# First tiles of K: one tile's statistics early, tile 0 split from TensorE's bank, tokens normalized in place, and another closing of the block

## The chip, the cores and the metric

The kernel runs on one core of one Trainium2 chip. The metric is the device time of one execution in microseconds, lower is better. All numbers below are of the kernel before the change.

## The reference

One transformer layer on 2048 tokens of width 512: a linear attention with 32 heads of 64, then a mixture of 8 experts of which each token takes two. The change touches the first part, the normalization of the tokens and the projection and accumulation of K.

```python
def attn(x, Wq, Wk, Wv, Wo, bo):              # x: [2048, 512], already normalized
    q = relu(x @ Wq); k = relu(x @ Wk); v = x @ Wv      # [2048, 32 * 64]
    kv = einsum('bhsd,bhse->bhde', k, v)                # sum over the tokens
    qkv = einsum('bhsd,bhde->bhse', q, kv)
    normalizer = clip(einsum('bhsd,bhd->bhs', q, k.sum(axis=tokens)), 1e-06, None)
    return (qkv / normalizer) @ Wo + bo

x = x + attn(layernorm(x), ...)               # layernorm: (x - mean) / sqrt(var + 1e-5)
x = x + moe(layernorm(x), ...)                # gates: softmax of the top 2 of 8 scores
# moe: h = silu(x @ w1[e].T + b1[e]); y = h @ w2[e].T + b2[e]; out = sum of gate * y
```

## The kernel before, in words

The tokens lie in 16 tiles of 128 tokens by 512. Everything is float32, and TensorE takes each product as three matmuls of rounded halves: each operand is split into a rounded part (`_hi`, made by ScalarE) and the difference to it (`_lo`, made by VectorE), and `three` (lines 1633 to 1636) issues hi x hi, hi x lo and lo x hi.

Instead of V and K'V the kernel accumulates A = xn' K over the tokens, and multiplies by Wv later. K has 2048 columns, taken in four chunks of 512. For each tile in a chunk, `project_k` (line 1652) gives 12 matmuls into a bank of pK, ScalarE and VectorE make k_hi and k_lo of it, and `accumulate_at` (line 1663) adds 12 matmuls to the four banks of pA. The first chunk also makes the operands: per tile VectorE takes statistics (`stats`: BATCH_NORM_STATS2 and BATCH_NORM_AGGREGATE), ScalarE the root (`sqrt_var`), VectorE refines its reciprocal in four small steps (`newton_rstd`) and normalizes (`normalize`, line 1206). TensorE transposes the tile into the bank pT (`transpose_xn`, line 1644), ScalarE copies it to xnT (`put_xnT`) and rounds the copy (`split_xnT`), VectorE subtracts. ScalarE and VectorE also split the untransposed tile (`split_xn`) and blocks of Wk (`split_wk`).

The order on every engine is written out by hand, with semaphores between the engines. For the first chunk `chunk0_pair` (line 1688) gives TensorE's order: project tile n + 1, transpose tile n + 2, accumulate tile n. Pairs 1 to 6 are a loop on TensorE (line 1703), pairs 0 and 7 stand apart. VectorE's order at the start is in lines 1256 to 1269, ScalarE's in lines 864 to 883. `keep_clock` issues transposes whose result nobody reads.

The normalized tile goes to xn_new (two buffers), and GpSimd copies it back over the tile in xn (`keep_xn`, line 587), which xn_kept tells. ScalarE's `split_xn` waits for that copy; VectorE waits for the copy and the transposes of the tile two before, ahead of writing the buffer again (line 1213).

SyncE's queue loads tile 0 of the tokens (semaphore s_first), four blocks of Wk, then tiles 1 to 3 (all on s_x[0], line 418), three small tensors of biases (s_b), and the other twelve tiles.

At the other end the experts' results are added to the output by GpSimd's DMAs (`add_out`, line 711, 39 of them, the last from y_last); SyncE waits for the last two of each parity (lines 563 and 564). The block (`nc.Block()`, line 396) closes with a drain on each engine and a barrier of all five.

## Time and profile before

| | us |
|---|---|
| median of 3 runs | 1025.12 (1024.0 to 1026.88) |
| profiled execution, its own time | 1023.68 |
| its span, first to last instruction | 1021.7 |
| TensorE busy | 998.7 |
| VectorE, ScalarE, GpSimd busy | 689.6, 515.1, 267.5 |
| granted TensorE clock, mean | 0.996 |

Busy time of TensorE counts overlapping matmuls once; a matmul of 512 columns is shown as 0.39 long, and one starts 0.23 after the other. A name such as pA<-k_hi,xn_hi is output<-inputs. In brackets stands how long the engine was idle ahead of the row and what ended it. PEq, POOLq and SPq are the sequencers of TensorE, GpSimd and SyncE; drains, semaphore instructions and branches are theirs and count as no busy time.

### The profile page before, as it was taken

What the parts mean: (1) busy time and instruction counts of PE and PEld (TensorE: products, weight loads), DVE (VectorE), ACT (ScalarE), POOL (GpSimd) and SP (SyncE); (2) the same over time, 40 slices, a digit from 0 to 9 for tenths busy, and PEclk for the clock granted to TensorE, in tenths of its full rate; (3) what the DMA queues carried; (4) which work ended last, traced back from release to release, by engine and by line L of the source; (5) the groups of instructions that cost most, each with busy time, mean ns of one, the idle gap of its engine ahead of it and who ended that gap; (6) DMA issues with size and microseconds to landing.
All of it is one profiled execution on the core that took longest, in us unless ns stands there. A gap on an engine that the chain in (4) does not pass through costs nothing.

```text
span 1021.7 us, 17596 instructions
## 1 busy us (share of the span) xinstructions
PE 998.7 (98%) x5029; PEld 841.5 (82%) x5030; DVE 689.6 (68%) x1555; ACT 515.1 (50%) x1325; POOL 267.5 (26%) x432
## 2 busy tenths in 40 slices
PE   8999999999999999999999999999999989999995
PEld 7777888888888888888788888888888879989984
DVE  6888665565566667667877887788877754444442
ACT  4445444444444447755555555555555953333331
POOL 2000000000000002223323333333224645555553
PEclk9999999999999999999999999999999999999998
DMA  7012500100000011343111111111136725565642
GB/s 259 1 41 82 206 21 21 41 21 21 21 21 22 21 63 63 103 172 114 49 45 52 41 41 41 41 41 43 39 100 183 207 64 100 106 104 100 113 90 33
DMA packets 46858, 75.31 MB, mean 74 GB/s; under 512 B 6089, under 2 KB 18554, under 8 KB 46690
## 3 DMA queue, kind: packets, MB, share of 16 engines
q1 hardware_dynamic: 37010, 56.04, 17.7%
q0 software_dynamic: 9808, 18.79, 10.0%
q8 instruction: 18, 0.29, 0.1%
q14 instruction: 22, 0.18, 0.1%
HBM read 53.14 MB, written 23.50 MB: 75 GB/s over the span
## 4 chain that ended last, share of the span: by engine, by line
PE 90%; DVE 5%; ACT 2%; issue 1%; DMA 1%; SPq 0%; POOLq 0%; ACTq 0%; DVEq 0%
PE pK L1634 15%; PE pK L1636 15%; PE pK L1635 15%; PE pA L1634 6%; PE pA L1635 6%; PE pA L1636 6%; PE pX L1634 6%; PE pX L1636 5%; PE pX L1635 5%; PE pA L1769 3%; PE pT L1979 2%; PE pT L1715 2%; PE pA L1903 1%; PE pX L1997 1%; PE pK L1903 1%
## 5 line engine op out<-in xcount | busy, mean ns | idle before, releaser
L983 ACT ACTIVATE qs<-q,nrec 128x64 f32<-128x64 f32 x512 | 129.6, 335 | 89.0 <-DVE nrec L1359 89.0
L1634 PE MATMUL pA<-k_hi,xn_hi 128*128 128x512 f32 x256 | 101.2, 395 | 1.2 <-DVE xn_lo L1217 0.7
L1634 PE MATMUL pK<-wk_hi,xnT_hi 128*128 128x512 f32 (+1 forms) x256 | 100.0, 391 | 0.7 <-DVE xnT_lo L1217 0.7
L1634 PE MATMUL pK<-wq_hi,xnT_hi 128*128 128x512 f32 x256 | 100.4, 392 | 0.0
L1636 PE MATMUL pK<-wq_hi,xnT_lo 128*128 128x512 f32 x256 | 99.9, 390 | 0.0
L1635 PE MATMUL pA<-k_lo,xn_hi 128*128 128x512 f32 x256 | 99.8, 390 | 0.0
L1635 PE MATMUL pK<-wk_lo,xnT_hi 128*128 128x512 f32 (+1 forms) x256 | 99.7, 390 | 0.0
L1636 PE MATMUL pA<-k_hi,xn_lo 128*128 128x512 f32 x256 | 99.7, 389 | 0.0
L1636 PE MATMUL pK<-wk_hi,xnT_lo 128*128 128x512 f32 (+1 forms) x256 | 99.6, 389 | 0.0
L1635 PE MATMUL pK<-wq_lo,xnT_hi 128*128 128x512 f32 x256 | 99.6, 389 | 0.0
L1634 PE MATMUL pX<-m_hi,qsT_hi 128*128 128x512 f32 x240 | 99.0, 413 | 0.0
L1636 PE MATMUL pX<-m_hi,qsT_lo 128*128 128x512 f32 x240 | 94.2, 392 | 0.0
L1635 PE MATMUL pX<-m_lo,qsT_hi 128*128 128x512 f32 x240 | 93.7, 390 | 0.0
L1352 DVE TENSOR_TENSOR qs<-q,ksum 128x512 f32<-128x512 f32 x64 | 51.8, 810 | 55.1 <-ACT q L977 55.1
L603 POOL TENSOR_TENSOR wv_lo<-wv_in,wv_hi 128x512 fp32r<-128x512 f32 x4 | 5.2, 1293 | 313.6 <-ACT wo_hi L904 313.6
L727 POOL DMA_INDIRECT out<-y,slot_token x38 | 65.8, 1732 | 69.4 <-DVE y L1600 44.1
L1237 DVE SCALAR_TENSOR_TENSOR k_lo<-pK,k_hi 128x512 fp32r<-128x512 f32 x64 | 44.1, 689 | 56.4 <-ACT k_hi L853 56.4
L847 ACT CAST xn_hi<-xn 128x512 fp32r<-128x512 f32 x64 | 39.6, 619 | 67.5 <-PE pA L1636 67.4
L977 ACT ACTIVATE q<-pK 128x512 f32<-128x512 f32 x64 | 38.2, 597 | 67.8 <-PE pK L1636 67.7
L853 ACT ACTIVATE k_hi<-pK 128x512 fp32r<-128x512 f32 x64 | 38.0, 594 | 66.5 <-PE pK L1636 66.5
L1158 ACT ACTIVATE hT<-pX,b1T 128x128 f32<-128x128 f32 (+1 forms) x117 | 34.1, 363 | 72.0 <-PE pX L1997 72.0
L1217 DVE TENSOR_TENSOR xn_lo<-xn,xn_hi 128x512 fp32r<-128x512 f32 x64 | 45.6, 712 | 27.4 <-ACT xn_hi L847 27.4
(283 smaller groups left out, 2464.7 us busy)
## 6 DMA issues: line engine op xcount, KB each, us to landing
w_in<-in_ffn_w SPq DMA_DIRECT2D x22, 256.0 KB, 3.6
w_in<-in_ffn_w SPq DMA_DIRECT2D x8, 704.0 KB, 7.4
xn<-in_attn_hidden_states SPq DMA_DIRECT2D x16, 256.0 KB, 5.9
wv_in<-in_attn_Wv SPq DMA_DIRECT2D x16, 256.0 KB, 2.7
wo_in<-in_attn_Wo SPq DMA_DIRECT2D x16, 256.0 KB, 2.9
wk_in<-in_attn_Wq SPq DMA_DIRECT2D x4, 1024.0 KB, 5.7
xnT_dram<-xnT SPq DMA_DIRECT2D x4, 1024.0 KB, 11.5
x_in<-in_attn_hidden_states SPq DMA_DIRECT2D x16, 256.0 KB, 2.6
```

The costliest lines, as they stand in the source:

```text
L727: pool.indirect_dma_start(out, bass.IndirectOffsetOnAxis(slot_token[:, i:i + 1].bitcast(U32), 0), rows, None, bounds_check=T - 1, oob_is_e ...
L847: nc.scalar.copy(xn_hi[:, b * D:(b + 1) * D], xn[:, ds(t * D, D)]).then_inc(xn_hi_ready, 1)
L853: nc.scalar.activation(k_hi[:, b * CW:(b + 1) * CW], pK[:, b * 512:(b + 1) * 512], ACT.Relu).then_inc(k_hi_ready, 1)
L977: nc.scalar.activation(q[:, b * CW:(b + 1) * CW], pK[:, b * 512:(b + 1) * 512], ACT.Relu).then_inc(q_ready, 1)
L983: i = nc.scalar.activation(qs[:, s], q[:, s], ACT.Copy, scale=nrec[:, b * HC + h:b * HC + h + 1])
L1158: last = nc.scalar.activation(hT[0:w, b * P:(b + 1) * P], pX[0:w, b * P:(b + 1) * P], ACT.Silu, bias=b1T[0:w, ds(b * E + e, 1)])
L1217: return nc.vector.tensor_tensor(dst, src, f(hi), ALU.subtract)
L1237: nc.vector.scalar_tensor_tensor(out=k_lo[:, s], in0=pK[:, b * 512:(b + 1) * 512], scalar=0.0, in1=f(k_hi[:, s]), op0=ALU.max, op1=ALU.sub ...
L1352: nc.vector.tensor_tensor(qs[:, b * CW:(b + 1) * CW], q[:, b * CW:(b + 1) * CW], ksum[:, c * CW:(c + 1) * CW], ALU.mult).then_inc(qk_ready, 1)
L1634: nc.tensor.matmul(dst, lhs[0], rhs[0], start=start, stop=False)
L1635: nc.tensor.matmul(dst, lhs[0], rhs[1], start=False, stop=False)
L1636: return nc.tensor.matmul(dst, lhs[1], rhs[0], start=False, stop=stop)
```

## The change

1. Tile 1 gets a semaphore of its own (s_second), and s_x[0] counts tiles 2 and 3 alone. VectorE takes tile 1's statistics between the third and the fourth block of Wk, and normalizes it behind the fourth. Tile 2's statistics and its normalization are parted in the same way, around tile 1's xnT_lo.
2. Tile 0: ScalarE rounds xnT_hi from the bank pT, VectorE takes the difference from the bank, and ScalarE's copy to xnT comes after both.
3. All tiles are normalized in place in xn. xn_new, GpSimd's copy and the semaphore xn_kept are gone; TensorE transposes from xn, and ScalarE waits for xn_ready.
4. TensorE transposes the biases ahead of tile 1 instead of behind it, and its loop over pairs 1 to 6 becomes straight code.
5. The block is made with `no_gpsimd_drain=True`. GpSimd waits for the last adds itself and issues `dma_reset()`. In the built program that is a drain marked as a reset, which names the semaphores 96 to 255; the other engines' drains now stand ahead of the barrier's own instructions, and GpSimd has none but the reset.

```diff
-    xn_new = sb("xn_new", 2 * D, 168 * KB)
...
+        s_second = sem("s_second")
...
-        xn_kept = sem("xn_kept")
...
-        block = ctx.enter_context(nc.Block())
+        block = ctx.enter_context(nc.Block(no_gpsimd_drain=True))
...
-                    sp.dma_start(xn[:, t * D:(t + 1) * D], x[t * P:(t + 1) * P, :]).then_inc(s_x[g] if t else s_first, 16)
+                    sp.dma_start(xn[:, t * D:(t + 1) * D], x[t * P:(t + 1) * P, :]).then_inc(s_x[g] if t > 1 else (s_first, s_second)[t], 16)
...
-            def keep_xn(t, b):
-                pool.wait_ge(xn_ready, t + 1)
-                pool.tensor_copy(xn[:, ds(t * D, D)], xn_new[:, b * D:(b + 1) * D]).then_inc(xn_kept, 1)
...
-            keep_xn(0, 0)
-            keep_xn(1, 1)
-            keep_xn(2, 0)
-            keep_xn(3, 1)
-            with pool.Fori(2, NT // 2) as p:
-                for b in range(2):
-                    keep_xn(2 * p + b, b)
...
+            pool.wait_ge(s_add[0], 16 * (NS // 2 + 1))
+            pool.wait_ge(s_add[1], 16 * (NS // 2))
+            pool.dma_reset()
...
             split_wk(0, 1)
+            act.wait_ge(xnT_put, 1)
+            nc.scalar.copy(xnT_hi[:, 0:D], pT[:, :]).then_inc(xnT_hi_ready, 1)
+            split_wk(0, 2)
+            act.wait_ge(xnT_lo_ready, 1)
             put_xnT(0)
-            split_xnT(0, 0, 0)
-            split_wk(0, 2)
             split_wk(0, 3)
             sqrt_var(1)
-            act.wait_ge(xn_kept, 1)
+            act.wait_ge(xn_ready, 1)
...
-                    act.wait_ge(xn_kept, n + 1)
+                    act.wait_ge(xn_ready, n + 1)
...
             def layernorm1(t, b):
                 stats(xn[:, ds(t * D, D)], t)
+                normalize1(t)
+
+            def normalize1(t):
                 newton_rstd(t)
-                if not (isinstance(t, int) and t < 2):
-                    dve.wait_ge(xnT_put, t - 1)
-                    dve.wait_ge(xn_kept, t - 1)
-                normalize(xn_new[:, b * D:(b + 1) * D], xn[:, ds(t * D, D)]).then_inc(xn_ready, 1)
+                normalize(xn[:, ds(t * D, D)], xn[:, ds(t * D, D)]).then_inc(xn_ready, 1)
...
-            split_xnT(0, 0, 0)
+            dve.wait_ge(xnT_hi_ready, 1)
+            lo(xnT_lo[:, 0:D], pT[:, :], xnT_hi[:, 0:D]).then_inc(xnT_lo_ready, 1)
             split_wk(0, 2)
+            dve.wait_ge(s_second, 16)
+            stats(xn[:, D:2 * D], 1)
             split_wk(0, 3)
-            dve.wait_ge(s_x[0], 48)
-            layernorm1(1, 1)
+            normalize1(1)
             split_xn(0, 0, 0)
             split_k(0, 0)
-            layernorm1(2, 0)
+            dve.wait_ge(s_x[0], 32)
+            stats(xn[:, 2 * D:3 * D], 2)
             split_xnT(1, 1, 1)
+            normalize1(2)
             add_k(0, 0, 0)
...
-                    last = nc.tensor.transpose(pT[:, i * P:(i + 1) * P], xn_new[:, b * D + i * P:b * D + (i + 1) * P], ident[:, :])
+                    last = nc.tensor.transpose(pT[:, i * P:(i + 1) * P], xn[:, t * D + i * P:t * D + (i + 1) * P], ident[:, :])
...
-            transpose_xn(1, 1)
             pe.wait_ge(s_b, 48)
...
+            transpose_xn(1, 1)
...
-            with pe.Fori(1, 7) as p:
+            for p in range(1, 8):
                 chunk0_pair(p)
-            chunk0_pair(7)
```

ScalarE at the start of the program, before; rs is the scratch of the root, wk_in a raw block of Wk:

```order
L834 COPY xnT<-pT 128x512 [waits xnT_put]
L842 CAST xnT_hi<-xnT 128x512 [waits xnT_ready]
L826 CAST wk_hi<-wk_in 128x512 [waits s_wk02]
L826 CAST wk_hi<-wk_in 128x512 [waits s_wk03]
L830 ACTIVATE rs<-mv,eps 128x1 [waits var_ready]
L847 CAST xn_hi<-xn 128x512 [waits xn_kept]
```

ScalarE at the same place in the changed program:

```order
L860 CAST xnT_hi<-pT 128x512 [waits xnT_put]
L817 CAST wk_hi<-wk_in 128x512 [waits s_wk02]
L825 COPY xnT<-pT 128x512 [waits xnT_put,xnT_lo_ready]
L817 CAST wk_hi<-wk_in 128x512 [waits s_wk03]
L821 ACTIVATE rs<-mv,eps 128x1 [waits var_ready]
L838 CAST xn_hi<-xn 128x512 [waits xn_ready]
```

The rounding of tile 0 stands first and reads pT; the copy to xnT has moved behind the third block of Wk and waits for VectorE's difference.

VectorE from its first difference of tile 0 to the k_lo of tile 0, before; the BN rows are statistics, the rows on rs refine the reciprocal:

```order
L1217 TENSOR_TENSOR xnT_lo<-xnT,xnT_hi 128x512 [waits xnT_hi_ready]
L1217 TENSOR_TENSOR wk_lo<-wk_in,wk_hi 128x512 [waits wk_hi_ready] x2
L1200 BN_STATS st_117<-xn 128x6 [waits s_x0]
L1203 BN_AGGR mv<-st_117 128x2 [waits bn_stats_done]
L1190 RECIPROCAL rs<-rs 128x1 [waits sqrt_ready]
L1192 TENSOR_SCALAR rs<-mv,rs 128x1 [waits rstd_step]
L1194 TENSOR_SCALAR rs<-rs 128x1 [waits rstd_step]
L1196 TENSOR_SCALAR rs<-rs 128x1 [waits rstd_step]
L1206 TENSOR_SCALAR xn_new<-xn,mv,rs 128x512 [waits rstd_step]
L1217 TENSOR_TENSOR xn_lo<-xn,xn_hi 128x512 [waits xn_hi_ready]
L1237 SCALAR_TENSOR_TENSOR k_lo<-pK,k_hi 128x512 [waits k_hi_ready]
```

VectorE at the same place in the changed program:

```order
L1210 TENSOR_TENSOR xnT_lo<-pT,xnT_hi 128x512 [waits xnT_hi_ready]
L1210 TENSOR_TENSOR wk_lo<-wk_in,wk_hi 128x512 [waits wk_hi_ready]
L1193 BN_STATS st_116<-xn 128x6 [waits s_second]
L1196 BN_AGGR mv<-st_116 128x2 [waits bn_stats_done]
L1210 TENSOR_TENSOR wk_lo<-wk_in,wk_hi 128x512 [waits wk_hi_ready]
L1183 RECIPROCAL rs<-rs 128x1 [waits sqrt_ready]
L1185 TENSOR_SCALAR rs<-mv,rs 128x1 [waits rstd_step]
L1187 TENSOR_SCALAR rs<-rs 128x1 [waits rstd_step]
L1189 TENSOR_SCALAR rs<-rs 128x1 [waits rstd_step]
L1199 TENSOR_SCALAR xn<-xn,mv,rs 128x512 [waits rstd_step]
L1210 TENSOR_TENSOR xn_lo<-xn,xn_hi 128x512 [waits xn_hi_ready]
L1230 SCALAR_TENSOR_TENSOR k_lo<-pK,k_hi 128x512 [waits k_hi_ready]
```

Tile 1's statistics have moved ahead of the fourth block of Wk and wait for s_second; the four rows on rs and the normalization stay behind it, and the normalization writes xn itself.

TensorE between the projection and the first accumulation of tile 0, before:

```order
L1635 MATMUL pK<-wk_lo,xnT_hi 128x512
L1636 MATMUL pK<-wk_hi,xnT_lo 128x512
L1649 MATMUL pT<-ident,xn_new 128x128 [waits xnT_ready,xn_ready]
L1649 MATMUL pT<-ident,xn_new 128x128 x3
L1682 MATMUL pX<-ident,gw_in 128x8 [waits s_b]
L1682 MATMUL pX<-ident,gw_in 128x8 x3
L1685 MATMUL pX<-ident,b_in 128x8 x2
L1685 MATMUL pX<-ident,b_in 96x8
L1686 MATMUL pX<-ident,b_in 128x32
L1634 MATMUL pA<-k_hi,xn_hi 128x512 [waits k_lo_ready,xn_lo_ready]
```

TensorE at the same place in the changed program:

```order
L1632 MATMUL pK<-wk_lo,xnT_hi 128x512
L1633 MATMUL pK<-wk_hi,xnT_lo 128x512
L1678 MATMUL pX<-ident,gw_in 128x8 [waits s_b]
L1678 MATMUL pX<-ident,gw_in 128x8 x3
L1681 MATMUL pX<-ident,b_in 128x8 x2
L1681 MATMUL pX<-ident,b_in 96x8
L1682 MATMUL pX<-ident,b_in 128x32
L1646 MATMUL pT<-ident,xn 128x128 [waits xnT_ready,xn_ready]
L1646 MATMUL pT<-ident,xn 128x128 x3
L1631 MATMUL pA<-k_hi,xn_hi 128x512 [waits k_lo_ready,xn_lo_ready]
```

The transposes of the biases (gw_in, b_in) come first, and tile 1's, which wait for VectorE, directly ahead of the accumulation.

## Rows read from the trace of the kernel before

**Rows 1.** The page: span, and busy time of each engine over it.

```profile
span 1021.7 us, 17596 instructions
PE 998.7 (98%) x5029; PEld 841.5 (82%) x5030; DVE 689.6 (68%) x1555; ACT 515.1 (50%) x1325; POOL 267.5 (26%) x432
```

**Rows 2.** Instructions of the block's end, line 227: engine, operation, duration ns, start us.

```profile
L227 POOLq DRAIN  x1: 9617/9617/9617, 1011.8 to 1011.8; - x1
L227 SPq COMPARE_BRANCH  x1: 38/38/38, 1014.7 to 1014.7; - x1
L227 POOLq EVENT_SEMAPHORE  x2: 17/17/17, 1021.5 to 1021.6; - x2
```

**Rows 3.** SyncE's own waits from 1000 us on: total us, times, longest.

```profile
SPq L227 <- PEq L227: 6.7, 1, 6.7
```

**Rows 4.** Instructions of the program's start, line 2053, on GpSimd's queue.

```profile
L2053 POOLq INC_SWDGE_SEM  x1: 31/31/31, 0.2 to 0.2; - x1
L2053 POOLq DRAIN  x1: 174/174/174, 0.4 to 0.4; - x1
```

**Rows 5.** Section 6 of the page: GpSimd's DMA issues by tile, with counts.

```profile
xg<-xn_dram,slot_token POOLq DMA_INDIRECT x39, 4.2
out<-y,slot_token POOLq DMA_INDIRECT x38, 4.9
meta_dram<-vals,slot_i POOLq DMA_INDIRECT x32, 2.6
```

**Rows 6.** Timeline of the first tiles: start us, us, engine, line, operation, count, idle before.

```profile
7.15 0.59 ACT L834 COPY xnT<-pT 128x512 f32<-128x512 f32 x1 [0.28 <-PE pT L1649]
7.77 0.62 ACT L842 CAST xnT_hi<-xnT 128x512 fp32r<-128x512 f32 x1
8.42 0.69 DVE L1217 TENSOR_TENSOR xnT_lo<-xnT,xnT_hi 128x512 fp32r<-128x512 f32 x1 [0.45 <-ACT xnT_hi L842]
9.17 0.50 PE L1634 MATMUL pK<-wk_hi,xnT_hi 128*128 128x512 f32 x1 [0.74 <-DVE xnT_lo L1217]
10.70 0.69 DVE L1200 BATCH_NORM_STATS2 st<-xn 128x6 f32<-128x512 f32 x1 [0.38 <-DMA xn<-in_attn_hidden_states]
12.42 0.59 ACT L853 ACTIVATE k_hi<-pK 128x512 fp32r<-128x512 f32 x1
12.99 0.55 DVE L1206 TENSOR_SCALAR xn_new<-xn,mv,rs 128x512 f32<-128x512 f32 x1
13.59 0.66 PE L1649 MATMUL pT<-ident,xn_new 128*128 128x128 f32 x4 [1.41 <-DVE xn_new L1206]
14.05 0.68 DVE L1237 SCALAR_TENSOR_TENSOR k_lo<-pK,k_hi 128x512 fp32r<-128x512 f32 x1
14.88 0.47 PE L1634 MATMUL pA<-k_hi,xn_hi 128*128 128x512 f32 x1
```

**Rows 7.** Busy time in one stretch: length, PE, PEld, DVE, ACT, POOL, clock, DMA share, GB/s.

```profile
9.00:10.00 1.00, 0.83 (x4) 0.70 (x5) 1.00 (x3) 0.43 (x1) 0.00 (x0) 1.00 1.07 377
```

**Rows 8.** Timeline of TensorE in the first chunk of K, transposes and accumulations.

```profile
24.44 0.50 PE L1634 MATMUL pA<-k_hi,xn_hi 128*128 128x512 f32 x1
36.09 0.60 PE L1649 MATMUL pT<-ident,xn_new 128*128 128x128 f32 x4
36.83 0.50 PE L1634 MATMUL pA<-k_hi,xn_hi 128*128 128x512 f32 x1
42.45 0.60 PE L1649 MATMUL pT<-ident,xn_new 128*128 128x128 f32 x4
42.89 0.50 PE L1634 MATMUL pA<-k_hi,xn_hi 128*128 128x512 f32 x1
98.77 0.50 PE L1634 MATMUL pA<-k_hi,xn_hi 128*128 128x512 f32 x1
```

**Rows 9.** Timeline around one copy by GpSimd, VectorE's difference beside it.

```profile
29.30 0.62 POOL L589 COPY xn<-xn_new 128x512 f32 x1 [5.46 <-DVE xn_new L1206]
29.64 0.81 DVE L1217 TENSOR_TENSOR xn_lo<-xn,xn_hi 128x512 fp32r<-128x512 f32 x1
```

## The prediction

> **What bounds the kernel now.** I read the page first: the span is 1021.7 us and TensorE is busy for 998.7 of it [rows 1]. So nothing that another engine does in the middle can be worth much, and what TensorE does not fill has to be found at the two ends and in waits. The instructions of the block's last line come next, since the span does not end with the last computation: GpSimd's queue holds a DRAIN of 9617 ns from 1011.8, and the barrier that closes the program follows it at 1021.5 [rows 2]. SyncE has seen all adds to the output land by 1014.7, when it branches to the end [rows 2]; it then waits 6.7 us for the barrier [rows 3]. That view names TensorE as the releaser; what came last is the drain. The third view is the timeline of the first tiles, where the reader is to see ScalarE copy the transposed tile twice, one after the other, before TensorE starts on K at 9.17, and VectorE start tile 1's statistics only at 10.70, when three tiles are in, with the first accumulation at 14.88 behind them [rows 6]. The fourth is TensorE in the first chunk of K: transposes at 36.09 and 42.45, accumulations at 36.83 and 42.89 [rows 8]. The first of those two starts 0.74 after its transposes, the second 0.44: every other step waits for VectorE.
>
> My sum is made against the profiled execution's own time, 1023.68 us (its span and 1.98 around it). The median of the three runs shown is 1025.12, 1.44 above it; I take the sum off both alike.
>
> **Tile 0 split from TensorE's bank.** Before, the transposed tile is copied to SBUF in 0.59, the copy rounded in 0.62, and VectorE's difference starts at 8.42, 0.69 long [rows 6]. Now ScalarE rounds straight from the bank and VectorE subtracts from the bank. I give both the durations of the nearest rows (0.59 for a read of that bank by ScalarE, 0.68 for VectorE's reading of a bank in the k_lo row). TensorE starts about 0.64 earlier, at 8.53. The copy to SBUF is still made, but behind the difference, and nobody waits for it before tile 1's transposes. By itself this is worth nothing: the accumulation waits for tile 1's statistics too, as they stand ahead of xn_lo and k_lo on VectorE.
>
> **Tile 1's statistics early.** They wait for one tile, not three. Three were in at 10.70 less a few hundredths [rows 6]; the queue moves 377 GB/s then [rows 7], 0.70 us for a tile of 262,144 bytes, so tile 1 should be in two tiles earlier, near 9.28. From statistics to normalization VectorE needs 12.99 - 10.70 = 2.29 [rows 6]; the fourth block of Wk is now subtracted in between, in about 0.6, most of it while ScalarE takes the root, which I count as 0.2. Normalization starts at 9.28 + 2.29 + 0.2 = 11.77, 1.22 before 12.99. xn_lo, k_lo and the accumulation follow as before, if k_hi is there: it came 12.42 - 9.17 = 3.25 behind TensorE's start [rows 6], so now at 11.8 to 11.9 and 0.59 long, ahead of k_lo at 12.83. TensorE has the bias transposes and tile 1's (0.66 us [rows 6]) done by then. First accumulation: 14.88 - 1.22 = 13.66. Behind it VectorE takes tile 2's statistics, tile 1's xnT_lo, then normalizes tile 2; its end near 16.5 meets TensorE, free 2.85 after 13.66. So the 1.2 us stays. Bounds: nothing, if tile 1 lands with tile 3; 1.5 us, if it is in by 9.0. I take 1.2. POOL's copy of tile 0, for which ScalarE's xn_hi waited, is gone as well, but was done long before.
>
> **Normalized in place.** Fifteen more steps lose GpSimd's copy. Its row matters because it overlaps VectorE's xn_lo: the copy runs from 29.30 to 29.92, and the difference from 29.64 takes 0.81 against 0.69 for one that no copy meets [rows 9, 6]. [...] That difference ends a chain: from transposes at 36.09 to the accumulation after next at 42.89 are 6.80, and from 36.83 to the next transposes at 42.45 are 5.62 [rows 8]; 6.80 + 5.62 = 12.42 is the period of a pair, and (98.77 - 24.44) / 6 = 12.39 the measured one [rows 8]. With 0.13 less in the chain a pair takes 12.27. TensorE's own work, 2 x (5.62 + 0.44) = 12.12, stays below that. Six pairs give 6 x 0.13 = 0.8 us. Bounds: 0, if the normalization in place pays it back; 1.6 (6 x 0.27), if the chain falls under TensorE's own work. The waits that VectorE drops before normalizing had been met earlier.
>
> **TensorE's loop unrolled.** Steps 1 to 7 of the pair loop become straight code. Accumulations keep their distance over the loop's edges (the measured pair is the chain's), so the branch costs nothing that shows: 0. SyncE's queue keeps its order and its issues.
>
> **Closed without a drain.** The plain drain goes. In its place GpSimd waits for the adds (in at 1014.7) and then does a reset, of a form that the trace does not have. Of the 9.6 us, 1011.8 to 1014.7 are cover for the transfer and stay; 6.7 are not [rows 2, 3]. A drain with no DMA behind it took 0.17 at the start [rows 4]; the one at the end follows 109 and two more DMAs [rows 5], so its 6.7 us may be some 60 ns for each. The reset costs between 0.17 and 6.7. I take 1.0, near the lower row, because what it could wait for has landed. Saved: 5.7 us.
>
> **Sum.** 1.2 + 0.8 + 5.7 = 7.7. Profiled execution: 1023.68 - 7.7 = 1016.0, span 1014.0. Median of runs: 1025.12 - 7.7 = 1017.4.
>
> **Rivals.** (1) The reset costs what the drain cost, or the clearing of the queue's records moves behind the span into the 1.98 us around it. For it: the 60 ns per DMA may be bookkeeping that any ending must do. Against it: the reset is issued when nothing is outstanding. Saved 1.2 + 0.8 = 2.0, time 1023.1: no change. [...]
> (2) Slower: the reset does the drain's walk and clears semaphores one by one besides. With 6.7 for the walk and 31 ns for each of the 160 semaphores that the built reset names, the length of the one instruction on semaphores of that queue [rows 4], it takes 11.7, 5.0 over the drain; less 2.0 from the front that is 1028.1. It turns slower once the reset exceeds 6.7 + 2.0 = 8.7. Against it: it would have to cost more than what it replaces.
> (3) The front doesn't move, because tile 1 lands late or TensorE, with VectorE's new order, waits for the fourth block of Wk (due there at 10.9, ready near 10.9): saved 0.8 + 5.7 = 6.5, time 1018.6. The range of the forecast covers it.
>
> **Chances.** A measurement of this kernel can tell about 0.3%, 3.1 us, from no change. My forecast, with (3) inside it: 0.80, from 1015.5 (reset 0.17, front 1.5, chunk 1.5, a microsecond of scatter) to 1021.5 (reset 3, front 0.5). Rival (1): 0.16. Rival (2): 0.04. Faster by over 0.3%: 0.80; within: 0.16; slower: 0.04. The range from 1015.0 to 1022.5 leaves out a good part of (1), all of (2) and the edges of the first.
>
> **What would show it.** On GpSimd's queue one DRAIN that starts after the last landing, about 2.9 us after where the old one started, and lasts 1.0; the span ends 0.3 behind it. First projection matmul near 8.5, first accumulation near 13.7, statistics of tile 1 near 9.3. xn_lo at 0.69 throughout, no copy on GpSimd, the pair at 12.27 and the last transposed step's accumulation near 96.8. A reset over 4 us, or a time around the span far above 1.98, would make the forecast wrong; so would new idle time of TensorE in the unrolled steps.

## The result, and the profile after

The changed kernel takes 1015.14 us (median of 4 runs, 1014.65 to 1015.29) against 1026.0 us for the kernel before beside it (4 runs, 1024.0 to 1027.16). The ratio is 0.990, 95% interval 0.9886 to 0.9914. The profiled execution took 1015.22 us, 8.46 less than that of before, with 1.72 us around its span. I had forecast 1016.0 for it and 1017.4 for the median, with a range from 1015.0 to 1022.5: the measured median lies only 0.14 above the range's lower end.

The page of the changed kernel, to be read against [rows 1]: the span is 8.2 us shorter, and TensorE is busy for the same time.

```profile
span 1013.5 us, 17496 instructions
...
PE 998.8 (99%) x5029; PEld 841.7 (83%) x5030; DVE 686.7 (68%) x1555; ACT 515.4 (51%) x1325; POOL 256.4 (25%) x416
```

The end comes first, since the largest term was there. These are instructions by source line (engine queue, operation, count, duration in ns, start in us). The reset on line 806 answers to the DRAIN of [rows 2]:

```profile
L806 POOLq DRAIN  x1: 293/293/293, 1013.0 to 1013.0; - x1
...
L226 POOLq EVENT_SEMAPHORE  x2: 17/17/17, 1013.3 to 1013.4; - x2
...
L226 SPq COMPARE_BRANCH  x1: 43/43/43, 1013.0 to 1013.0; - x1
```

VectorE's last work, first in the kernel before and then in the changed one:

```profile
1010.51 0.75 DVE L1628 TENSOR_SCALAR y_last<-pA,slot_gate 128x512 f32<-128x512 f32 x1 [1.74 <-PE pA L1636]
```

```profile
1008.72 0.75 DVE L1625 TENSOR_SCALAR y_last<-pA,slot_gate 128x512 f32<-128x512 f32 x1 [1.74 <-PE pA L1633]
```

It starts 1.79 us earlier, so 1.8 us of the 8.2 come from the front and the middle. The remaining 6.4 come from the end: the reset starts when the last add is in, lasts 0.29 us, and the barrier follows at 1013.3, where the old drain held it until 1021.5.

The timeline of the first tiles, against [rows 6]:

```profile
9.06 0.50 PE L1631 MATMUL pK<-wk_hi,xnT_hi 128*128 128x512 f32 x1
...
9.53 0.69 DVE L1193 BATCH_NORM_STATS2 st<-xn 128x6 f32<-128x512 f32 x1
...
11.93 0.55 DVE L1199 TENSOR_SCALAR xn<-xn,mv,rs 128x512 f32<-128x512 f32 x1
...
12.99 0.68 DVE L1230 SCALAR_TENSOR_TENSOR k_lo<-pK,k_hi 128x512 fp32r<-128x512 f32 x1
...
13.82 0.47 PE L1631 MATMUL pA<-k_hi,xn_hi 128*128 128x512 f32 x1 [0.52 <-DVE k_lo L1230]
```

TensorE starts on K at 9.06 (9.17 before), tile 1's statistics at 9.53 (10.70), its normalization at 11.93 (12.99), and the first accumulation at 13.82 (14.88), 1.06 earlier. This is one pair of executions. The five profiled executions with this front (the changed kernel, e2, e3, e9, e10) have the first accumulation at 13.10 to 14.21, the five with the old front (before, e1, e4, e5, e8) at 14.88 to 15.64.

TensorE's accumulations in the first chunk, against [rows 8], and VectorE once beside them:

```profile
23.50 0.50 PE L1631 MATMUL pA<-k_hi,xn_hi 128*128 128x512 f32 x1
...
32.90 0.18 DVE L1196 BATCH_NORM_AGGREGATE mv<-st 128x2 f32<-128x6 f32 x1 [0.54 <-DVE st L1193]
...
36.19 0.50 PE L1631 MATMUL pA<-k_hi,xn_hi 128*128 128x512 f32 x1 [0.54 <-DVE xn_lo L1210]
...
42.12 0.48 PE L1631 MATMUL pA<-k_hi,xn_hi 128*128 128x512 f32 x1
...
97.51 0.50 PE L1631 MATMUL pA<-k_hi,xn_hi 128*128 128x512 f32 x1
```

From 42.12 to 97.51 the pairs take 12.25 to 12.28 us, as forecast. The first full pair, 23.50 to 36.19, takes 12.69: TensorE waits 0.54 for xn_lo, because VectorE stood still for 0.54 before it aggregated its statistics at 32.90, with no releaser but its own last instruction. At the end of the chunk the changed kernel is 98.77 - 97.51 = 1.26 ahead, and it stays 1.25 to 1.27 ahead until 717 us.

The rest of the 1.8 appears where the expert stage begins. This row of before and the one of the changed kernel are the same transposes of w_in; "issue" means that TensorE waited for nothing that the profile shows:

```profile
817.48 0.63 PE L1903 MATMUL pK<-ident,w_in 128*128 128x128 f32 x4 [1.23 <-issue]
```

```profile
815.66 0.63 PE L1899 MATMUL pK<-ident,w_in 128*128 128x128 f32 x4 [0.29 <-issue]
```

TensorE's unexplained wait shrinks from 1.23 to 0.29. At VectorE's last work the changed kernel is 1.79 ahead, 0.53 more than in the stages before this one.

### The profile page after: what moved, and what is told of

It reads as the page before. It is cut to its first block, busy times and chain, and to the rows that moved or that the text cites. A ratio compares the mean times of both kernels' runs of the same rounds, so it can differ in the third digit from the quotient of the medians.

```text
span 1013.5 us, 17496 instructions
## 1 busy us (share of the span) xinstructions
PE 998.8 (99%) x5029; PEld 841.7 (83%) x5030; DVE 686.7 (68%) x1555; ACT 515.4 (51%) x1325; POOL 256.4 (25%) x416
## 3 DMA queue, kind: packets, MB, share of 16 engines
HBM read 53.14 MB, written 23.50 MB: 76 GB/s over the span
## 4 chain that ended last, share of the span: by engine, by line
PE 91%; DVE 5%; ACT 2%; issue 1%; DMA 0%; POOL 0%; ACTq 0%; DVEq 0%; POOLq 0%
PE pK L1631 15%; PE pK L1633 15%; PE pK L1632 15%; PE pA L1631 6%; PE pA L1632 6%; PE pA L1633 6%; PE pX L1631 6%; PE pX L1633 5%; PE pX L1632 5%; PE pA L1765 3%; PE pT L1975 2%; PE pT L1711 2%; PE pA L1899 1%; PE pX L1993 1%; PE pK L1899 1%
## 6 DMA issues: line engine op xcount, KB each, us to landing
wk_in<-in_attn_Wq SPq DMA_DIRECT2D x4, 1024.0 KB, 5.8
xnT_dram<-xnT SPq DMA_DIRECT2D x4, 1024.0 KB, 11.7
```

## The experiments

Time is the median over the runs; the interval is that of the ratio to the kernel before, run on the same chip alongside. The kernel before itself came to 1025.13 (23 runs, 1023.28 to 1028.51) beside e1 to e4, 1024.64 (23 runs, 1023.13 to 1026.88) beside e5 to e8, and 1024.77 (9 runs) beside e9 to e12. The letters A to I name the theories in the expectation that stands ahead of each result.

```
                                     time us   range               runs  ratio interval
e1  before, only the end changed     1018.14   1016.70 to 1019.65   6    0.9910 to 0.9946
e2  changed, plain drain back        1020.82   1020.31 to 1022.27   6    0.9936 to 0.9970
e3  changed, waits and plain drain   1022.55   1021.87 to 1024.44  12    0.9965 to 0.9988
e4  before, only in place            1023.80   1022.11 to 1024.98  12    0.9973 to 0.9996
e5  before, only the loop unrolled   1024.48   1022.44 to 1025.33  12    0.9983 to 1.0004
e6  changed, statistics 1 late       1017.39   1015.84 to 1018.47   6    0.9915 to 0.9940
e7  changed, tile 0 through SBUF     1014.78   1014.71 to 1015.04   4    0.9888 to 0.9917
e8  before, TensorE kept busy        1024.74   1022.92 to 1025.03  11    0.9990 to 1.0007
e9  changed, drains in the loop      1020.85                        1    (profiled run)
e10 changed, no reset                1014.40   1013.98 to 1014.93   5    0.9884 to 0.9915
e11 e6, TensorE kept busy            1015.83   1015.24 to 1016.38   5    0.9897 to 0.9928
e12 e7, no reset, tile 1 first       1014.78   1014.40 to 1015.73   5    0.9889 to 0.9921
```

### The end: e1, e2, e3, e9, e10

**e1, the kernel before with only its end changed.**

```diff
-        block = ctx.enter_context(nc.Block())
+        block = ctx.enter_context(nc.Block(no_gpsimd_drain=True))
...
                 add_out(i)
+            pool.wait_ge(s_add[0], 16 * (NS // 2 + 1))
+            pool.wait_ge(s_add[1], 16 * (NS // 2))
+            pool.dma_reset()
```

> The kernel before with only its end changed: GpSimd waits for the adds, resets its DMA state, and the block closes without the plain drain. Theory A (the three parts add up, the end is worth what the two traces differ by there): SyncE's branch to the barrier is followed by 0.3 to 0.5 us instead of 6.7, so the span falls by 6.4, from 1021.7 to about 1015.3, and the time of an execution like the profiled one from 1023.7 to 1017.3. The first 1008 us are as before. Rival B (the scatter of the kernel before, 1024.0 to 1027.2, sits in its drain, whose length varies): the median falls by more than 6.4, from 1026.0 to about 1017.3, and the runs lie within 0.7 us. Rival C (the scatter sits elsewhere): the median falls by 6.4, to 1019.6, and the runs stay 3 us apart.

Measured: span 1015.0 in the profiled execution, against 1015.3 expected, and 7.0 off the median. The rows by source line:

```profile
L818 POOLq DRAIN  x1: 303/303/303, 1014.5 to 1014.5; - x1
...
L227 POOLq EVENT_SEMAPHORE  x2: 17/17/17, 1014.8 to 1014.9; - x2
...
L227 SPq COMPARE_BRANCH  x1: 43/43/43, 1014.5 to 1014.5; - x1
```

The reset takes 0.30 here too, and the end alone is worth 6.4 to 7.0. But the runs stay 3 us apart, so B falls: most of the scatter of the kernel before is not in its drain. With it comes a clue, TensorE's mean granted clock of each run:

```
e1 runs, us (clock): 1016.70 (1.0)   1016.73 (1.0)   1017.89 (0.998)
                     1018.39 (0.997) 1018.53 (0.997) 1019.65 (0.995)
```

**e2, the changed kernel with the plain drain back** (the reverse edit).

> The changed kernel with only its end undone: plain drain, no waits for the adds, no reset. Theory A: the drain on GpSimd's queue starts near 1010 and lasts 9.6 us again, the span is 1013.5 + 6.4 = 1019.9, the time 1021.6, 2.1 below the profiled execution of before and 4 below its median if the drain varies from run to run as before does (then up to 1025). Rival D (the early part of the change also shortens the drain, because GpSimd has 16 copies fewer behind it): drain under 8 us, time below 1020.5.

Measured: 1020.82, 5.7 above the changed kernel; the profiled execution is the longest of the six (1022.27, 7.05 above the one of the changed kernel). The drain and what follows the branch are as before (D falls):

```profile
L226 POOLq DRAIN  x1: 9722/9722/9722, 1010.6 to 1010.6; - x1
L226 SPq COMPARE_BRANCH  x1: 38/38/38, 1013.6 to 1013.6; - x1
```

**e3, the two waits kept, but a plain drain behind them.**

```diff
             pool.wait_ge(s_add[1], 16 * (NS // 2))
-            pool.dma_reset()
```

(and `nc.Block()` as before.)

> The changed kernel with its two waits for the adds kept, and a plain drain where the reset was. The drain now starts when all has landed, at 1013.0. Theory E (a plain drain does a fixed piece of work for the DMAs of the program, about 60 ns for each, whenever it is issued): 9.6 us long, span 1023, time 1024.5 to 1025. Theory F (that work went on beside the landing only in part: the 6.7 us begin when the last transfer lands): 6.7 us long, span 1020.1, time 1021.8, as without the waits. Rival G (what made the drain long was that it was issued with a transfer in flight; the waits cure it, not the reset): 0.3 us long, span 1013.5, time 1015.2 as the changed kernel.

Measured: 1022.55, 7.4 above the changed kernel.

```profile
L226 POOLq COMPARE_BRANCH  x1: 41/41/41, 1012.7 to 1012.7; - x1
...
L226 POOLq DRAIN  x1: 7835/7835/7835, 1012.9 to 1012.9; - x1
```

Everything has landed at 1012.7, and the plain drain still takes 7.8. So G falls: it is the kind of closing, not the waiting, that is cheap. The number lies between E and F: of the drain's own work of 7.8 us about 1.1 ran beside the transfer in the kernel before, where 6.7 stayed uncovered [rows 2, 3]. The twelve runs of e3 spread over 2.6 us at mean clocks of 0.995 and 0.996, where those of the changed kernel spread over 0.6. So some scatter comes back with the plain drain as well; which part of the program it sits in, no profile here shows.

**e9, plain drains in the routing loop as well.**

```diff
                     put_slots(2 * h + (b - 2), b)
+                    pool.drain()
```

(the end as in e2.)

> The changed kernel with the plain drain at the end again and no waits or reset, and twelve plain drains more on GpSimd, one behind the two DMAs of each step of the routing loop, where GpSimd then idles for 7 us. The last drain comes behind 111 DMAs in all and 83 since the drain before it. Theory A (about 60 ns for each DMA issued since the last drain): the drains in the loop last for their two DMAs' landing and little more, all alike, 2 to 2.5 us, and the last one's uncovered part falls from 6.7 to 83 x 0.06 = 5.0. Theory B (60 ns for each DMA ever issued): the drains in the loop grow by 0.12 us from one to the next, 1.4 us over the twelve, and the last is as long as before, 9.6. Theory C (a fixed price for any plain drain that has had a software DMA before it, whatever their number): each lasts 8 to 10 us, the loop's idle time does not hide them, and the time goes up by 10 us or more.

Measured, the twelve drains of line 688 (shortest, median, longest) and the end:

```profile
L688 POOLq DRAIN  x12: 3399/3939/8017, 517.3 to 779.6; - x12
...
L226 POOLq DRAIN  x1: 8454/8454/8454, 1010.4 to 1010.4; - x1
L226 SPq COMPARE_BRANCH  x1: 38/38/38, 1013.4 to 1013.4; - x1
```

The drains in the loop have two DMAs each to wait for. In order they take 3.9, 3.6, 3.6, 4.0, 3.4, 3.8, 3.6, 4.3, 4.3, 4.6, 5.0 and 8.0 us, so C, a fixed price of 8 to 10, falls. The last drain is uncovered from 1013.4 to 1018.9, 5.5 us, against 6.7 without the drains before it: by that B falls, and A (5.0) comes near. The last drain is shorter when earlier ones stand in the loop. But the drains in the loop are longer than I expected and not all alike: from the first to the eleventh they grow by 1.2 us, as much as B gives, and 5.5 is more than a strict proportion gives. It is a single run. That the drain's work is proportional to the DMAs since the last one is not shown, and why the twelfth is longest stays open.

**e10, no reset either.**

```diff
             pool.wait_ge(s_add[1], 16 * (NS // 2))
-            pool.dma_reset()
```

> The changed kernel without the reset: GpSimd waits for the adds and joins the barrier, with neither drain nor reset. Theory A: the reset's 0.29 us was all that stood between the last landing and the barrier, so the time falls by 0.2 to 0.3, to 1014.9. Rival B: SyncE's own way to the barrier (branch at 1013.0, its event at 1013.2) sets the end as much, and it falls by less than 0.15. Rival C: what the reset cleared is then cleared behind the span: the span falls by 0.3 and the time around it, 1.7 us, grows.

```profile
L226 POOLq EVENT_SEMAPHORE  x2: 17/17/17, 1012.8 to 1012.9; - x2
...
L226 SPq COMPARE_BRANCH  x1: 43/43/43, 1012.5 to 1012.5; - x1
```

From the branch to the span's end it is 0.5 us with and without the reset (1013.0 to 1013.5, 1012.5 to 1013.0). B holds: SyncE's own way to the barrier hides most of the 0.29. The time around the span is 1.73, as with the reset (1.72), so C falls. The median is 0.74 below the changed kernel's, which was not run beside it; but in the profiled execution the branch itself comes 0.5 earlier: that difference does not lie at the end. The ratio to before, 0.9884 to 0.9915, is that of the changed kernel.

### The first tiles and the scatter: e6, e7, e8, e11, e12

**e6, tile 1's statistics late again.**

```diff
+            split_wk(0, 3)
             dve.wait_ge(s_second, 16)
+            dve.wait_ge(s_x[0], 32)
             stats(xn[:, D:2 * D], 1)
-            split_wk(0, 3)
             normalize1(1)
```

> The changed kernel with only tile 1's statistics put back behind the fourth block of Wk and behind the landing of all of the first four tiles. Theory A (my term for the early statistics): normalization of tile 1 near 13.0, first accumulation near 14.9, 1.1 later than in the changed kernel, time of a good execution 1016.2. Theory C (the kernels with the old first tiles lie up to 4 us apart in their runs and show a lower mean clock in the slower ones, because TensorE idles for 1.4 us before tile 1's transposes and sometimes loses its clock there): the scatter comes back, 1016.2 to 1019, mean clock 0.995 to 0.999, median near 1017.5. Rival D (the scatter belongs to tile 0's way through SBUF, TensorE's idle 0.74 before the first projection): no scatter here, runs within 0.7 us.

Measured: first accumulation at 15.09, 1.27 later than in the changed kernel, and the scatter is back; even the fastest run is 0.7 above the changed kernel's median. TensorE's rows with idle time, and its windows (length, busy, clock, DMA share, GB/s):

```profile
13.80 0.66 PE L1647 MATMUL pT<-ident,xn 128*128 128x128 f32 x4 [1.48 <-DVE xn L1199]
15.09 0.47 PE L1632 MATMUL pA<-k_hi,xn_hi 128*128 128x512 f32 x1 [0.64 <-DVE k_lo L1230]
...
15.00:16.00 1.00, 0.91 (x4) 0.91 1.05 385
16.00:17.00 1.00, 1.00 (x4) 0.50 1.06 389
17.00:18.00 1.00, 1.00 (x3) 0.50 1.09 375
18.00:20.00 2.00, 2.00 (x10) 0.69 1.06 370
```

This profile shows what those of before and of the changed kernel don't: TensorE is at 0.50 of full speed for 0.2 + 2.0 + 1.2 = 3.4 us from 15.8 on, after 1.48 us and 0.64 us of idling; from 20 on it is at 1.00 again. From 15.87 to 18.86 a matmul of 512 columns starts 0.42 to 0.43 us after the one before it; in e11, at 1.00, 0.22 to 0.24. I estimate the work lost at half of the 3.4, 1.7 us. In the profiles of before and e1, the clock is 1.00 in the same windows after idle stretches of 1.41 and 1.04. The kernel with only the loop unrolled (e5) shows it too, after 2.00 us:

```profile
14.35 0.66 PE L1649 MATMUL pT<-ident,xn_new 128*128 128x128 f32 x4 [2.00 <-DVE xn_new L1206]
...
16.00:17.00 1.00, 1.00 (x5) 0.80 1.07 391
17.00:18.00 1.00, 1.00 (x4) 0.50 1.08 360
18.00:20.00 2.00, 2.00 (x6) 0.50 1.06 375
```

**e11, e6 with that idle stretch filled** by ten transposes of the identity that nobody waits for.

```diff
+            keep_clock(10)
             transpose_xn(1, 1)
```

> The kernel of the late statistics (tile 1's statistics behind the fourth block and the four tiles), with ten more transposes of the identity for TensorE, 1.25 us, in the idle stretch before tile 1's transposes. Theory C (in the executions at 1016.6 to 1018.5 TensorE ran at half clock for about 3 us after that idle stretch): with the stretch filled the clock stays and the slow executions go: median 1015.9 instead of 1017.4, runs from 1015.6 to 1016.5, first accumulation still near 15.0. Rival D (the clock falls for another reason, or the idle 0.64 before the first accumulation is enough): median 1017 or more, with the half clock at 16 to 20 us still there.

```profile
13.79 0.66 PE L1647 MATMUL pT<-ident,xn 128*128 128x128 f32 x4 [0.45 <-DVE xn L1199]
...
16.00:17.00 1.00, 1.00 (x6) 1.00 1.06 387
17.00:18.00 1.00, 1.00 (x6) 1.00 1.09 365
18.00:20.00 2.00, 2.00 (x12) 1.00 1.06 373
```

The first accumulation is at 15.08, as in e6, but the clock stays up and the median falls by 1.56 to 1015.83. The two were measured on different chips, with five and six runs, and their ratio intervals touch (0.9897 to 0.9928 and 0.9915 to 0.9940). What supports C beside the medians is the mean clock: 0.999 to 1.0 in all five runs of e11, 0.997 to 0.999 in the six of e6. So for this kernel C is well supported: with the statistics late, most of what makes executions longer than 1016.4 is the half clock after the idle stretch. All runs of kernels with early statistics and the new closing show a mean clock of 0.998 to 1.0. The median of e11 is 0.69 above the changed kernel's, its profiled execution 1.16: that is what the later start costs with the clock kept.

Mean clocks can be compared only between kernels with the same end. In the kernel before, TensorE has nothing to do during the last drain, and its clock stands at 0.50 from 1015 us to the end, which counts in its 0.996.

**e8, the kernel before with the same filler.**

```diff
             project_k(0, 0, 0)
+            keep_clock(10)
             transpose_xn(1, 1)
```

> The kernel before with ten more transposes of the identity into the unused bank, about 1.25 us of work for TensorE, put where it idles 1.4 us before tile 1's transposes. Nothing waits for them. Theory C (the scatter is a clock lost in that gap): the best executions stay at 1023.3 to 1023.7, and the slow ones go: runs within 1 us, median 1023.8 instead of 1025.1. Rival D (gap before the first projection) or F (elsewhere, at 810 to 830): the runs stay spread over 3 to 5 us, median near 1025.

Measured: 1024.74, no better than before. TensorE's row before tile 1's transposes, the two that explain this execution's span of 1022.7, and windows:

```profile
13.63 0.66 PE L1649 MATMUL pT<-ident,xn_new 128*128 128x128 f32 x4 [0.31 <-DVE xn_new L1206]
...
412.70 0.62 ACT L903 CAST wv_hi<-wv_in 128x512 fp32r<-128x512 f32 x1 [1.27 <-DMA wo_in<-in_attn_Wo]
415.25 0.38 PE L1716 MATMUL pT<-at_hl,wv_hi 128*128 128x256 f32 x1 [0.80 <-POOL wv_lo L603]
...
18.00:20.00 2.00, 2.00 (x12) 1.00 1.06 371
```

The clock is 1.00 in these windows, yet the execution is 1.0 us longer than the profiled one of before. The microsecond is lost near 415: ScalarE waits 1.27 us for the load of a block of Wo before it rounds Wv's at 412.70 (411.53 in the profile of before), GpSimd's wv_lo behind it starts at 413.92 (412.75 there), as much later, and TensorE waits 0.80 for that. So there is a second source of scatter, a load that arrives just in time in the last part of the key and value stage. C is not shown for the kernel before by this run, since the median did not fall: none of its 11 runs is above 1025.03, where 7 of the 23 beside it of the kernel before are (1025.27 to 1026.88), but 7 of the 11 lie between 1024.5 and 1025.03, with mean clocks of 0.995 to 0.997.

**e7, tile 0 through its copy in SBUF again.**

```diff
-            act.wait_ge(xnT_put, 1)
-            nc.scalar.copy(xnT_hi[:, 0:D], pT[:, :]).then_inc(xnT_hi_ready, 1)
-            split_wk(0, 2)
-            act.wait_ge(xnT_lo_ready, 1)
             put_xnT(0)
+            split_xnT(0, 0, 0)
+            split_wk(0, 2)
```

(and VectorE's difference for tile 0 by `split_xnT(0, 0, 0)`.)

> The changed kernel with only tile 0 split from its copy in SBUF again. Theory A (worth nothing by itself): the first projection starts 0.6 later, near 9.7, the first accumulation stays at 13.8 since it waits for VectorE's k_lo and xn_lo, or comes up to 0.3 later because k_hi is later; time 1015.1 to 1015.4. Rival E (the split from the bank is on the path): first accumulation 0.6 later, time 1015.7. Rival D (the scatter comes from here): runs 3 us apart with a lower clock in the slow ones.

```profile
9.18 0.50 PE L1628 MATMUL pK<-wk_hi,xnT_hi 128*128 128x512 f32 x1 [0.74 <-DVE xnT_lo L1208]
...
13.95 0.47 PE L1628 MATMUL pA<-k_hi,xn_hi 128*128 128x512 f32 x1 [0.54 <-DVE k_lo L1228]
```

TensorE starts at 9.18, idles 0.74 before it, and the accumulation is still at 13.95. 1014.78 against 1015.14: the runs show no gain from the split. But the profiled execution of the changed kernel was an unfavourable one for it: tile 0's transposes took 1.06 us there, and TensorE started at 9.06. In e2, e3, e9 and e10, which split from the bank too, it started at 8.34 to 8.56. Where tile 1 was in early enough, tile 1's statistics then started at 9.02 (e3) and 8.79 (e9) and the first accumulation came at 13.32 and 13.10, up to 0.85 ahead of e7; where it was not (e2, e10), at 14.21 and 14.15. A gain of some tenths in a part of the executions is therefore not excluded.

**e12, an attempt to beat the changed kernel.**

```diff
                         for b in range(FB):
+                            if b == FB - 1:
+                                sp.dma_start(xn[:, D:2 * D], x[P:2 * P, :]).then_inc(s_second, 16)
```

(the outer loop then passes over tile 1; tile 0 is as in e7 and the end as in e10.)

> A kernel that might beat the changed one: tile 0 split from its copy in SBUF again (no slower in its run: 1014.8), no reset at the end, and tile 1 loaded before the fourth block of Wk instead of behind it. Theory A (first accumulation follows tile 1's statistics by 4.3 us): tile 1 lands 0.7 earlier, statistics start at 8.9 to 9.0 instead of 9.6, the first accumulation at 13.3 instead of 13.95, and with the reset's 0.25 the time is 1014.0. Rival B (the fourth block, now 0.7 later, makes TensorE wait inside the first projection, as it did for 0.61 us at 11.51 in the kernel with the plain drain back): first accumulation stays at 13.9, time 1014.6.

```profile
9.64 0.69 DVE L1194 BATCH_NORM_STATS2 st<-xn 128x6 f32<-128x512 f32 x1
...
13.94 0.47 PE L1631 MATMUL pA<-k_hi,xn_hi 128*128 128x512 f32 x1 [0.55 <-DVE k_lo L1231]
```

Neither theory: tile 1's statistics start at 9.64 just as in e7, with no idle time of VectorE before them. B's first accumulation and time came out, but not by its reason, since TensorE does not wait within the first projection. In these two executions the load is not what the statistics wait for; VectorE is, busy with tile 0's xnT_lo and the third block of Wk. That is not so in every execution. In e2, with tile 0 split from the bank, VectorE is free earlier and does wait for the load, and in e10 for 0.46:

```profile
9.90 0.70 DVE L1190 BATCH_NORM_STATS2 st<-xn 128x6 f32<-128x512 f32 x1 [0.80 <-DMA xn<-in_attn_hidden_states]
```

So the earlier load was tried where it could not help; together with the split from the bank it is untested. 1014.78 is e7's time. No version beats the changed kernel by more than the measurement can tell.

### The middle: e4, e5

**e4, the kernel before with only the normalization in place** (no copy by GpSimd; TensorE's loop has to be unrolled with it; first tiles and end untouched).

```diff
-                normalize(xn_new[:, b * D:(b + 1) * D], xn[:, ds(t * D, D)]).then_inc(xn_ready, 1)
+                normalize(xn[:, ds(t * D, D)], xn[:, ds(t * D, D)]).then_inc(xn_ready, 1)
```

> The kernel before with only the normalization in place: no second buffer, no copy by GpSimd, TensorE's pair loop unrolled as in the change. First tiles and end as before. Theory A: xn_lo takes 0.69 wherever it took 0.81, a pair of steps 12.26 instead of 12.39; over six pairs 0.8 us, less 0.4 if VectorE stalls once near 32 us as it did in the changed kernel. The first accumulation stays near 14.9 and the one near 98.8 comes 0.3 to 0.8 earlier; the span is 1021.2, the time 1023.1 against 1023.7. Rival H (the 0.6 us that the changed kernel gained between 717 and 1008 us belongs to this part): span 1020.5. Rival I (VectorE's wait near 32 us belongs to the early statistics, not to this part): no such wait here.

```profile
37.27 0.50 PE L1618 MATMUL pA<-k_hi,xn_hi 128*128 128x512 f32 x1 [0.51 <-DVE xn_lo L1201]
...
98.62 0.50 PE L1618 MATMUL pA<-k_hi,xn_hi 128*128 128x512 f32 x1
...
816.32 0.63 PE L1886 MATMUL pK<-ident,w_in 128*128 128x128 f32 x4 [0.20 <-issue]
```

Pairs take 12.24 to 12.29, except the first, 12.69, with the stall of VectorE again. So I falls. At 98.62 only 0.15 is gained; behind the expert stage's start, where TensorE's unexplained wait is 0.20, VectorE ends 1.1 earlier than before. H holds: that gain comes with this part, which has the unrolled loop in it; e5 parts the two.

**e5, the kernel before with only TensorE's loop unrolled.**

```diff
-            with pe.Fori(1, 7) as p:
+            for p in range(1, 8):
                 chunk0_pair(p)
-            chunk0_pair(7)
```

> The kernel before with only TensorE's loop over pairs of the first chunk written out; normalization still into the second buffer, with GpSimd's copies. Theory A (the 1.0 us that all kernels with this part gain between 812 and 838 us, where TensorE waits 1.2 us for nothing that the profile shows before the transposes of w_in, comes from the longer straight code of TensorE, which moves its later instructions): that wait falls from 1.2 to 0.2 or 0.3 and the end comes 0.6 to 1.0 earlier; pairs stay at 12.39, the accumulation near 98.8 stays, the time of an undisturbed execution is 1022.9 against 1023.7. Rival B (it comes from the normalization in place): the wait is 1.0 to 1.2 as before, the time 1023.7. As for the single wait of VectorE for 0.44 us near 32.5, after statistics: if the straight code causes it, it is here as well; if the copies that are gone do, it is not.

Measured: TensorE has no such wait before the transposes of w_in; its first idle row in the expert stage is the one that follows, of which 0.78 had been there before:

```profile
822.70 0.42 PE L1634 MATMUL pK<-w_hi,gT_hi 128*128 x1 [1.55 <-DVE gT_lo L1217]
```

A holds in its effect: straight code in the first chunk is enough to remove the wait of 1.23 us at 817. That it acts by moving the later instructions is not shown. The other profiles agree. With the loop the wait is 1.23 (before), 0.97 (e1) and 1.28 (e8); without it, it is 0.17 to 0.33 (changed kernel, e2, e3, e4, e9, e11, e12) or absent (e5, e6, e7, e10). The profiled execution had the half clock, but from GpSimd's first gather of the expert stage to its seventh it makes up 1.2 us on the profile of before (812.51 and 837.58 there for the starts of the DMAs, 815.44 and 839.28 here). The fastest run, 1022.44, is 0.7 under the fastest of before, 1023.13; the median shows no difference that can be told. VectorE's stall is absent here, as in before, e1 and e8. All kernels that normalize in place have it, at 32.1 to 34.0, and e6 and e11 at 96.9 and 95.3. In these two VectorE's program has one wait more and another order at the start; that this moves the stall is not shown.

## Why the prediction was right, step by step

**Closed without a drain (5.7, measured 6.4).** The mechanism was right and e1, e2 and e3 show it; the term was mis-sized. I gave the reset 1.0, from its two bounds of 0.17 and 6.7. It takes 0.29 and is mostly hidden by SyncE's way to the barrier (e10). The "some 60 ns for each" of 111 DMAs is 70 when nothing covers it (7.8 us, e3), and falls when earlier drains share it (e9). By single edits the end is worth 7.0 (e1, medians) and 5.7 (e2, medians). Rival (1) would have shown a span near 1019.7 and a median of 1023.1; the reset took 0.29, the span 1013.5. The time around the span went from 1.98 to 1.72, so nothing moved behind it; it is 1.75 in e4 and 1.77 in e2, with the plain drain, so it is not the reset that shortened it. Rival (2) needed a reset over 8.7.

**Tile 1's statistics early (1.2, measured 1.06).** Each time came 0.16 to 0.25 later than forecast (9.53 for 9.28, 11.93 for 11.77, 13.82 for 13.66). I derived 9.28 from the landing of tile 1. In the changed kernel's profile VectorE has no idle time ahead of 9.53, so its own work sets the start there; in e2 and e10 the load does, at 9.90 and 9.84, and in e9 tile 1 was in by 8.79. That the forecast lies within 0.25 of one execution is in part luck: the first accumulation moves by 1.1 us between executions of this front. What I missed is worth more than the term: without this part some executions lose TensorE's clock (0.50 for 3.4 us in e6's profile; 1.56 between the medians of e6 and e11). I took the 1.44 between the profiled execution and the median of before as scatter that would stay, and it did not: the changed kernel's median is 0.08 below its profiled execution. Of the 2.3 by which the forecast median was too high, 1.5 is this scatter and 0.8 the sum. How much of the scatter of the kernel before was the half clock stays open, since e8 kept the clock there and the median did not fall. The median came into the range by 0.14.

**Tile 0 split from the bank (0, no gain seen in the runs).** TensorE starts at 9.06, not 8.53. Tile 0's statistics started 0.28 later in this execution, and its transposes took 1.06 us. In e2 and e3 the start is at 8.56, as forecast. That nothing follows from it holds in the time of e7; in the profiles it depends on when tile 1 lands (e3 and e9 against e7).

**Normalized in place (0.8, measured 0.13 for each pair, 0.3 in the chunk).** xn_lo takes 0.68 to 0.69 throughout, where the profile of before has 0.80 or 0.81 from 29.64 on in the chunk, and the pair takes 12.27, exactly as worked out. The sum over six pairs lost 0.42 to one stall of VectorE that the profile of before has not. The 0.13 for each is 0.81 less 0.68, and the trace of before had it right.

**TensorE's loop unrolled (0, measured 0.5 to 1.2).** This step failed. I looked for the loop's branches where the loop is; the gain lies at 817 us, where TensorE waited 1.23 us for nothing visible. e5 shows the cause (the unrolled loop alone removes the wait); that the place of TensorE's later instructions does it was my estimate in e5 and is not shown.

So 7.7 became 8.2 in the span by errors that partly cancel: +0.7 at the end, -0.26 up to the second accumulation (0.94 earlier, 23.50 for 24.44), -0.48 in the pairs, +0.53 from the unrolled code; another 0.26 came off around the span. Rival (3), the front that doesn't move, falls, though one of its conditions does occur: in e2 and e10 TensorE waits 0.61 and 0.71 within the first projection for the difference of Wk's fourth block, and the first accumulation comes at 14.21 and 14.15, still 0.7 ahead of before.

## What to carry to other kernels

When GpSimd has issued many DMAs, look at the last drain and at what it takes behind the last landing. Here, behind 111 of them, waiting for the transfers and resetting instead costs 0.3 us where the plain drain costs 6.7 to 7.8. Profile more than one execution of the same front before a term of some tenths is called right or nothing. Read the granted clock of every run, not only of the profiled one, and among kernels with the same end: its mean was 0.997 to 0.999 in e6, 0.999 to 1.0 in e11, and the profile of e6 had 3.4 us at half speed behind an idle stretch, which is the place to look; e8 shows that long runs can have another cause. An edit to code that runs before 100 us (e5) removed a wait of 1.23 us at 817, so compare idle rows without a releaser along the whole trace.

## What the runs showed of the hardware that I had not expected

- A plain drain on GpSimd behind 111 DMAs, all landed, takes 7.8 us; a reset in its place 0.29 to 0.30.
- TensorE ran 3.4 us at 0.50 of its clock after idling 1.48 + 0.64 us (e6) and 2.00 us (e5), and not after 1.41 (before), 1.04 (e1) or 1.67 us (e4). The clock fell when TensorE was busy again. Of the 23 runs of the kernel before beside e1 to e4, ten form a group at 1023.3 to 1024.3 with a mean clock of 0.996, and thirteen reach up to 1028.5 at 0.992 to 0.995.
- VectorE stands still once, for 0.47 to 0.54 us, in all kernels here that normalize in place, at 32 to 34 us or at 95 to 97 us; no row shows what it waits for.
